# A mixture-of-experts stage and its seam: a normalisation moved ahead of a power on GpSimd, a bias product of 128 rows, fill products and an exponential behind the last item

## What is computed

```python
def _L2_ffn_ref(hidden, router_w, router_b, sw1, sb1, sw2, sb2, rw1, rb1, rw2, rb2):
    router_probs = softmax(flat @ router_w + router_b)
    topk_probs, topk_idx = top_k(router_probs, 2)
    weights = zeros_like(router_probs).at[arange(T)[:, None], topk_idx].add(topk_probs)
    shared_out = gelu(flat @ sw1 + sb1) @ sw2 + sb2
    h1 = gelu(einsum('td,edh->teh', flat, rw1) + rb1[None])
    expert_out = einsum('teh,ehd->ted', h1, rw2) + rb2[None]
    mixed = einsum('ted,te->td', expert_out, weights)
    return shared_out + mixed
...
x = x + _L2_ffn_ref(_layernorm(x), ...)
x = x + _L3_attn_ref(_layernorm(x), ...)
```

## Time and profile before

| | |
|---|---|
| three runs | 1907.52, 1921.55 and 1907.14 us |
| median | 1907.52 us |
| the profiled execution, its own time | 1917.72 us |
| its span (first to last instruction) | 1915.9 us |
| mean granted TensorE clock over the span | 0.887 of full speed |
| busy over the span | TensorE 81%, VectorE 64%, ScalarE 42%, GpSimd 34% |
| experts' block in the trace | from about 1123 to 1295 us |

### The profile page before, as it was taken

How to read it: one execution, slowest core, us unless ns; L and a number is a source line. 1 busy time by engine, 2 the same in 40 slices (tenths; PEclk the granted TensorE clock), 3 DMA queues, 4 the chain that set the end, 5 groups by cost and what they waited for, 6 DMA issues and landing times. The chain is left out here.

```text
span 1915.9 us, 34034 instructions
## 1 busy us (share of the span) xinstructions
PE 1561.4 (81%) x12089; PEld 1043.2 (54%) x12141; DVE 1223.1 (64%) x4221; ACT 812.5 (42%) x1746; POOL 659.2 (34%) x784
## 2 busy tenths in 40 slices
PE   4369666788868998857699989998867797999788
PEld 2137443455536777755334347665545664777555
DVE  6867556567277898844556534356848866999532
ACT  2233137166424877753155543336643400333332
POOL 4613320441014445430644032233112117777121
PEclk8676688799968999978899999998988958999999
DMA  2000000421015767640532000013110000000000
GB/s 89 0 12 1 10 31 0 112 70 33 1 60 201 250 216 293 235 167 7 156 87 52 11 18 7 23 44 82 43 65 1 1 1 1 2 3 2 2 1 23
DMA packets 81336, 115.58 MB, mean 60 GB/s; under 512 B 8464, under 2 KB 62608, under 8 KB 80400
## 3 DMA queue, kind: packets, MB, share of 16 engines
q0 software_dynamic: 18432, 67.38, 10.0%
q1 hardware_dynamic: 61008, 45.23, 8.6%
q10 hardware_dynamic: 1728, 0.79, 0.2%
HBM read 88.79 MB, written 1.05 MB: 47 GB/s over the span
## 5 line engine op out<-in xcount | busy, mean ns | idle before, releaser
L2911 POOL DMA_INDIRECT f_rows<-tree_table,f_index x128 | 129.5, 1012 | 185.3 <-PE f_ps_y L3112 77.7
L3112 PE MATMUL f_ps_y<-f_rows,shared_sb 128*128 128x128 f32 x1024 | 129.5, 289 | 31.3 <-ACT f_rows L3184 31.3
L3184 ACT ACTIVATE f_rows<-f_rows,f_low_act 128x128 f32<-128x128 f32 x512 | 152.9, 387 | 0.8
L3112 PEld LDWEIGHTS f_ps_y<-f_rows,shared_sb 128*128 128x128 f32 x1024 | 124.7, 203 | 37.3 <-ACT f_rows L3184 33.8
L1732 ACT ACTIVATE x_probs<-x_ps_z 128x768 f32<-128x768 f32 (+1 forms) x128 | 117.4, 917 | 60.5 <-PE x_ps_z L1590 42.0
L3011 DVE CUSTOM_DVE_ANT_0 f_rows<-f_rows,f_xn 128x128 f32<-128x128 f32 x512 | 111.2, 285 | 23.4 <-DMA f_rows<-tree_table,f_index 23.4
L88 POOL TENSOR_TENSOR rstd<-moments,shared_sb 128x4 f32<-128x4 f32 (+4 forms) x23 | 4.8, 207 | 329.4 <-DVE moments L66 329.1
L1417 DVE TENSOR_REDUCE x_minus_max<-x_ps_s 128x4 f32<-128x1024 f32 x64 | 78.1, 1224 | 62.0 <-PE x_ps_s L1590 61.9
L2397 ACT ACTIVATE f_hT<-f_ps_h,weights 128x512 f32<-128x512 f32 x72 | 49.4, 687 | 72.9 <-PE f_ps_h L2286 72.9
L3627 ACT ACTIVATE r_probs<-r_ps_z 128x768 f32<-128x768 f32 x64 | 51.9, 810 | 58.5 <-PE r_ps_z L3507 58.5
L2221 DVE SCALAR_TENSOR_TENSOR x_tokens<-f_ps_y,f_chosen,x_tokens 128x128 f32<-128x128 f32 x128 | 36.0, 344 | 62.3 <-PE f_ps_y L2299 61.8
(11 more groups left out here) (688 smaller groups left out, 4119.1 us busy)
## 6 DMA issues: line engine op xcount, KB each, us to landing
x_queries<-x_pieces SPq DMA_DIRECT2D x96, 64.0 KB, 2.1
x_keys<-x_pieces SPq DMA_DIRECT2D x84, 64.0 KB, 2.1
a_queries<-a_pieces SPq DMA_DIRECT2D x48, 64.0 KB, 2.1
a_keys<-a_pieces SPq DMA_DIRECT2D x48, 64.0 KB, 2.1
weights<-w_L_ffn SPq DMA_DIRECT2D x1, 2953.5 KB, 10.0
weights<-w_L_ffn SPq DMA_DIRECT2D x1, 2385.0 KB, 9.8
weights<-w_L_ffn SPq DMA_DIRECT2D x1, 2176.0 KB, 10.0
f_rows<-tree_table,f_index POOLq DMA_INDIRECT x128, 5.9
```

The lines of the kernel that those rows point to most:

```text
L2911: pool.indirect_dma_start(rows[:, place(u, j), tree, :], None, g.tree_table, bass.IndirectOffsetOnAxis(index[:, u % 2, low, j * TREES + tr ...
L3112: last = pe.matmul(ps_y[:, u % SUMS, j, :], g.ident, rows[:, place(u, j), tree, OUT + f * D:OUT + (f + 1) * D], start=False, stop=(low, j, ...
L3184: last = a.activation(row, row, ACT.Copy, scale=low_act[:, u % 3, j * TREES + tree, f:f + 1])
```

## The change

Four edits, all around the experts' block.

- GpSimd runs slots -18 to -15 (of which only -18 holds work, the two normalisations of the first sequence) ahead of its wait for the last `shifted` and of the last power, and the rest of the slots behind it.
- `chosenT` has 128 rows, all set to 1 at first, and `b2` has 128 rows, those from the tenth on zero. So the bias product runs over 128 rows. The weights' width in DRAM and in SBUF is the same, as every part is padded to 128 rows anyway.
- TensorE issues 14 fill products of 512 columns behind its last item.
- ScalarE takes an exponential of one column (of the constants that pad `probs`) behind its last item.

```diff
-        chosenT = sb("chosenT", [ITEMS, COLS])
+        chosenT = sb("chosenT", [P, COLS])
...
             for t in range(TURNS):
+                if t == TURNS - 1:
+                    for slot in range(att.first, FIRST_SLOT):
+                        run(slot)
                 pool.wait_ge(shifted, t + 1)
                 pool.tensor_tensor(probs[:, :, 0:E], euler[:, :, :], probs[:, :, 0:E], ALU.pow).then_inc(exped, 1)
...
-            for slot in range(att.first, att.behind):
+            for slot in range(FIRST_SLOT, att.behind):
                 run(slot)
             invert_part(pool, g, 1, MEASURED)
             invert_part(pool, g, 2, MEASURED)
...
                 for slot in slots_at(n, 1):
                     run(slot)
+            fill_wait(pe, g, ps_t[:, :], 512, 14)
...
                 for slot in slots_at(n, 0) + slots_at(n, 1):
                     run(slot)
+            a.wait_ge(padded, 1)
+            a.activation(exp_tried[:, :], probs[:, 0, E:E + 1], ACT.Exp)
...
-        "b2": np.concatenate([a["L2_ffn_rb2"], line("L2_ffn_sb2")], axis=0),
+        "b2": np.concatenate([a["L2_ffn_rb2"], line("L2_ffn_sb2"), np.zeros((P - 9, D), f)], axis=0),
```

More of the change, by code:

```diff
@@ L2132, in layer2_experts @@
         peak, total, scratch = sb("peak", [P, TILES]), sb("total", [P, TILES]), sb("scratch", [P, 1])
-        euler = sb("euler", [P, TILES, E])
+        euler, exp_tried = sb("euler", [P, TILES, E]), sb("exp_tried", [P, 1])
         top, chosen = sb("top", [P, TILES, 8]), sb("chosen", [P, 2, TILES, E])
         probs, rest = sb("probs", [P, TILES, E + 6]), sb("rest", [P, TILES, E + 6])
-        chosenT = sb("chosenT", [ITEMS, COLS])
+        chosenT = sb("chosenT", [P, COLS])
         hT = sb("hT", [P, 4, COLS])
```

## The result

| | before | changed | ratio, 95% interval |
|---|---|---|---|
| first comparison, 4 runs each | 1912.87 us | 1896.44 us | 0.9916 (0.9886 to 0.9945) |
| second comparison, 17 and 6 runs | 1909.46 us | 1894.57 us | 0.9923 (0.9895 to 0.9951) |

The forecast was 1895 us and 0.65% less; the time is 1896.4 us and 0.8% less. The direction and the order of size are right, and the change is within the 1% that was called hard to tell, though the intervals leave out no change at all. The median of before that the prediction started from, 1907.52 us, was of three runs and a low one: later runs of the same kernel have medians of 1912.45 us (24 runs, from 1907.29 to 1919.22), 1909.46 us (17 runs) and 1911.21 us (9 runs).

The account below looks back on a forecast made before the run. TensorE's pace bounds the experts' block; at the seam the chain is VectorE, GpSimd and the engines' meeting. Terms -2.8 - 5.7 - 3.9 = -12.4 us off the 1907.52 us median give 1895.1 us, range 1886 to 1908 us.

Parts of the forecast that it names:

- this sign: Prediction counts as wrong if the stages through the experts-to-attention seam plus three slots are not 12 us shorter.
- Step 1: Before GpSimd's last power: normalising the first sequence earlier removes TensorE's whole wait for it, -2.8 us.
- Step 2: Ninth item's down-products: a 128-row bias product runs at plain pace, 2.67 us instead of 4.11, -5.7 us in all.
- The rival that it would be no cheaper: Bias product: columns alone set its price, so 5.7 us fall away, total 1900.8 us; chance 0.11.
- Step 3: Seam after the experts: 14 fills cut TensorE's idleness to 1.1 us and keep full clock through slots 12-14, -2.6 us.
- a rival of its own: Seam: the clock falls despite the fills, only the table's 1.28 us remain, total 1897.7 us; chance 0.11.
- Step 4: Seam: an exponential behind ScalarE's last item hides the table load that slot 13 waits for, -1.28 us.
- What lies behind: Stages behind the experts' block and slots 12 to 14: the sum counted no gain or loss there.
- rival of clock won behind: Stages behind the experts win some clock, 7 us more, total 1888 us; chance 0.11.
- the 12.4 us of the sum: Whole kernel: normalisation 2.8, bias product 5.7 and seam 3.9 us saved together.

Follow-up runs that it names:

- e4: Kernel before, 9-row bias product issued first in every second tile so that two narrow products stand side by side; 1906.1 us, ratio 0.9968.
- e5: The changed kernel with all four edits, profiled again without any edit; 1894.6 us, ratio 0.9923 to the kernel before.
- e1: Kernel before with only the first sequence's normalisation moved ahead of the last power on GpSimd; 1904.6 us, ratio 0.9968.
- e2: Kernel before with only the bias product widened from 9 to 128 rows; 1903.4 us, ratio 0.9967.
- e10: The kernel before, profiled again without any edit; 1911.9 us in one run.
- e9: Kernel before with the bias product over 64 rows rather than 9 or 128; 1909.3 us, ratio 0.998.
- e3: Kernel before with only the 14 fill products and the exponential behind the last item; 1903.4 us, ratio 0.9961.
- e6: Changed kernel with 16 fills instead of 14, plus 2 and 1 behind the scores of slots 12 and 13; 1896.8 us, ratio 0.9931.
- e8: Changed kernel with 28 fill products instead of 14; 1886.5 us in two runs, ratio 0.9891 to the kernel before.
- e7: Changed kernel without its fill products; 1894.4 us, ratio 0.9928 to the kernel before.

## Why the prediction was right

**What bounds the kernel.** That the experts' block runs at TensorE's pace is confirmed by every run: what went out of TensorE's list came off the block to a tenth of a microsecond. The sum up to slot 12 was 2.8 + 4.3 + 1.4 = 8.5 us; 8.8 were measured, four times (157.35 to 157.37 against 166.18). The 0.3 us between them are the 0.1 us in each of three turns by which the up-product behind a narrow product was longer (e4): 2.82 + 3 x 1.55 + 1.35 = 8.8 us.

**Luck in the total.** The forecast of 1895 us is off by only 1.3 us because two errors are opposite. It started from a median that was 5.3 us below that of the first comparison (1907.52 against 1912.87), and the change won 16.4 us there and not 12.4. The prediction also said that it is wrong if the stages up to the seam and three slots are not 12 us shorter: they are 11.1 us shorter in the first profile, and 12.7 us in e5, where the clock was kept. Strictly, the first profile fails this sign.

**Step 1, the normalisation: -2.8 us.** 2.86 us measured in e1. What it missed is a second price. The prediction took it from the kernel's trace that an idle stretch of 2.82 us leaves the clock alone. Of six profiles that have this wait, two (e2 and e10) show a fall behind it, of some 1.6 us each. The edit is therefore worth about 2.9 us in some executions and, by these two profiles, 4.5 in others.

**Step 2, the bias product: -5.7 us.** The ninth item at 2.68 us and the last at 2.87 us are as forecast; what it missed is the 0.1 us behind each of the first three. The rival that it would be no cheaper fell with e2, and the reason was tested by itself in e4 and e9.

**Step 3, the fills: -2.6 us with the clock kept.** The fills' length, the tail that hides them and the gap (1.2 us, 1.1 forecast) came as said. That the clock is still at 2.4 GHz in slots 12 to 14 is true of e3, e5, e6 and e8 and false of the first profile of the changed kernel. The prediction held this as a rival of its own, with 1.28 us left of 3.9; in that profile it was in between, 2.3 us, since the clock fell later and came back sooner. Without the fills the slots took 6.15 us (e7), so the fills were worth 1.7 us where the clock was kept and 0.2 us in that profile, and no median shows them.

**Step 4, the exponential: -1.3 us.** The load moved under TensorE's last item, and 1.28 us went from slot 12 (e7).

**What lies behind: nothing.** This is the term that was off. Between the executions of before and after it is 4.1 us, and it is hardly chance alone: from slot 15 to the end the six profiles with the old seam take 611.9 to 612.2 us, but for one (e4) of 610.6; the six with the exponential ahead of the seam take 605.9 to 610.1. No instruction there is changed. What differs is the clock. The stretch behind the seam before, and the same in the changed kernel with the one that answers to the 55 us of the earlier trace rows:

```profile
1304.00:1915.00 611.00, 531.27 (x4742) 0.91 0.05 15
```

```profile
1288.00:1894.00 606.00, 523.61 (x4737) 0.93 0.05 15
1530.00:1585.00 55.00, 44.62 (x180) 0.71 0.00 1
```

The 55 us that stood at 0.53 stand at 0.71. From slot 15 on the granted clock was at half for 107.1 us in the kernel before and for 90.1 us in the changed one. Over the twelve profiles the length goes with that time: 610.0 to 612.2 us in the eight with 94 to 107 us at half clock, 605.9 to 608.0 us in the four with 80 to 90 us. The eight share a stretch of 10.2 us at half clock that begins 225 to 226 us behind slot 15; in the four none begins there.

So this is the prediction's rival of clock won behind, at some 2 to 6 us instead of 7, and of the size of the distance between the 12.4 us of the sum and the 14.9 and 16.4 us of the medians. Which edit moves the falls is not shown. The new seam alone doesn't: e3 has it and takes 610.0 us. Nor is it the clock kept at the seam: in e7 it falls there, and the rest takes 607.7 us. All four short ones hold the two edits of the experts and the exponential, but so does e6, with 610.1 us.

## What to carry to other kernels

A small product among full ones can cost more for changing the array's shape than for its own work (here 0.39 us for the two changes around it against 0.22 us for its two instructions at the plain pace): if its rows can be padded with zeros to the shape of its neighbours at no cost in memory or transfers, do so, and where not, put the small ones side by side. Work that is moved ahead of an instruction which waits is free only if that wait is longer than the work; read the idle time in front of the instruction that you pass (here 2.54 us for work of 1.59 us). And judge an edit of a few microseconds by the distance between two instructions that enclose it: here the edits of the experts were read to a tenth of a microsecond while the whole varied by twelve.

## What the runs showed of the hardware that was not expected

The spread between executions of one program is mostly that of the granted clock. Over the twelve profiles the span goes with its mean: 0.902 and 0.903 for 1883.6 and 1884.4 us, 0.887 and 0.883 for 1915.9 and 1923.2 us. It does so for one program too: the changed kernel took 1894.6 us at 0.894 and 1883.6 us at 0.902, the kernel before 1915.9 us at 0.887 and 1910.1 us at 0.892. The first Gelu of the experts came between 1113.1 and 1136.4 us, with the same work ahead of it in all twelve, but for the rows of `chosenT` that are set to 1 (0.514 us for 9 rows, 0.525 us for 128).

An idle stretch of one length may or may not lower the clock: the 2.82 us wait did so in two of six profiles. Nor was a gap of that length needed: behind the seam with the fills, where no gap is above 1.2 us, the clock fell in one profile of five.

A change of the array's shape costs 0.19 us in the mean of the changes into and out of it, for float32 products of 128 columns at full clock, whether the other shape has 9 or 64 rows.
